# A two-layer gated attention kernel on one core: its loads in the order of use, logarithms beside the first queries, and the ternary layer one unit earlier

## The reference

```python
x = x + tanh(g_xattn[0]) * L0_xattn(layernorm(x), ctx)          # 16 heads of 16, 77 keys
x = x + tanh(g_ffn[0]) * L0_ffn(layernorm(x), w1, w2)           # ternary weights, hidden 1024
x = x + tanh(g_xattn[1]) * L1_xattn(layernorm(x), ctx, distances, ...)
x = x + tanh(g_ffn[1]) * L1_ffn(layernorm(x), ...)              # expert 0, relu, hidden 1024, layer norm
```

## Time and profile before

| | us |
|---|---|
| median of 3 runs | 404.98 (404.76 to 409.9) |
| the profiled execution | 406.22 |
| its span in the trace | 404.5 |
| TensorE busy | 329.9 |
| VectorE busy | 282.7 |
| ScalarE busy | 283.5 |
| GpSimd busy | 230.9 |

### The profile page before, as it was taken

How to read it: one execution, slowest core, us unless ns; L and a number is a source line. 1 busy time by engine, 2 the same in 40 slices (tenths; PEclk the granted TensorE clock), 3 DMA queues, 4 the chain that set the end, 5 groups by cost and what they waited for, 6 DMA issues and landing times.

```text
span 404.5 us, 8923 instructions
## 1 busy us (share of the span) xinstructions
PE 329.9 (82%) x3222; PEld 271.4 (67%) x3222; DVE 282.7 (70%) x676; ACT 283.5 (70%) x516; POOL 230.9 (57%) x413
## 2 busy tenths in 40 slices
PE   2856878878866776878787899899877899999993
PEld 2646767667754453467566688788666799888882
DVE  6895568776777647989955557777856548666665
ACT  4366897799886777989934798866679755555550
POOL 4675644676577222457784755566775167444444
PEclk9996869998998868869999999999999999999998
DMA  8996431011100000320082222211100000000001
GB/s 242 278 179 170 92 86 41 10 39 43 42 6 17 2 0 2 52 25 2 2 257 53 50 53 53 52 35 27 45 2 2 2 0 29 28 28 27 28 28 52
DMA packets 23187, 22.02 MB, mean 54 GB/s; under 512 B 4711, under 2 KB 22504, under 8 KB 23067
## 3 DMA queue, kind: packets, MB, share of 16 engines
q1 hardware_dynamic: 23144, 21.45, 21.5%
HBM read 10.34 MB, written 2.10 MB: 31 GB/s over the span
## 4 chain that ended last, share of the span: by engine, by line
PE 46%; DVE 19%; ACT 17%; issue 10%; POOL 4%; DMA 3%; SPq 1%; ACTq 0%; POOLq 0%; DVEq 0%
PE psA L1723 10%; PE psA L1509 5%; PE psD L1707 5%; PE psBE L1707 4%; PE psD L1418 3%; ACT pp_hi L731 3%; DVE mx L1129 3%; PE psBE L1444 2%; DVE ham L1175 2%; DVE st L885 2%; ACT p L722 2%; PE psA L1493 2%; PE psA L1333 2%; DMA qb<-mT 2%; PE psA L1676 2%
## 5 line engine op out<-in xcount | busy, mean ns | idle before, releaser
L508 POOL TENSOR_TENSOR pp_lo<-p,pp_hi 124x512 f16<-124x512 f32 x80 | 92.7, 1178 | 46.6 <-ACT pp_hi L731 46.6
L404 POOL TENSOR_TENSOR lns<-lns,mhalf 128x2 f32<-128x2 f32 x39 | 31.0, 794 | 86.0 <-DVE lns L890 85.6
L1129 DVE TENSOR_REDUCE mx<-psBE 128x6 f32<-128x462 f32 (+1 forms) x96 | 54.5, 582 | 33.3 <-PE psBE L1444 32.9
L722 ACT ACTIVATE p<-psD 124x512 f32<-124x512 f32 x80 | 47.7, 597 | 27.8 <-PE psD L1418 27.1
L1418 PE MATMUL psD<-qb,ktb 98*124 98x256 f16 (+1 forms) x256 | 49.6, 291 | 12.1 <-DMA qb<-mT 10.3
L731 ACT ACTIVATE pp_hi<-p 124x512 f16<-124x512 f32 x80 | 50.4, 630 | 0.0
L1418 PEld LDWEIGHTS psD<-qb,ktb 98*124 98x124 f16 (+1 forms) x256 | 33.0, 145 | 16.9 <-DMA qb<-mT 13.2
L1444 PE MATMUL psBE<-kt_hi,q_hi 128*128 128x154 f16 (+2 forms) x160 | 34.0, 282 | 5.2 <-ACT mT L713 4.0
L1215 DVE TENSOR_TENSOR pp_lo<-space,pp_hi 128x512 f16<-128x512 f32 x32 | 25.7, 822 | 16.2 <-ACT space L834 15.5
L1723 PE MATMUL psA<-ew_hi,pp_hi 128*128 128x256 f16 x128 | 34.9, 273 | 0.0
L1723 PE MATMUL psA<-ew_hi,pp_lo 128*128 128x256 f16 x128 | 34.9, 273 | 0.0
(11 more groups left out here) (210 smaller groups left out, 1007.3 us busy)
## 6 DMA issues: line engine op xcount, KB each, us to landing
qb<-q_hi SPq DMA_DIRECT2D x32, 128.0 KB
xs<-in_x SPq DMA_DIRECT2D x8, 256.0 KB, 6.0
tw_raw<-in_tw SPq DMA_DIRECT2D x2, 1024.0 KB, 10.2
qb<-q_lo SPq DMA_DIRECT2D x16, 128.0 KB
space<-in_ew SPq DMA_DIRECT2D x2, 1024.0 KB, 6.5
out<-space SPq DMA_DIRECT2D x7, 256.0 KB, 2.1
ktb<-km SPq DMA_DIRECT2D x6, 248.0 KB, 7.9
qb<-bT_lo SPq DMA_DIRECT2D x8, 104.0 KB
```

What stands on the lines that cost most here:

```text
L508: nc.gpsimd.tensor_tensor(pl[:, u % 2, 2 * r:2 * r + 2, :], p32[:, n % 4, :, :], ph[:, u % 2, 2 * r:2 * r + 2, :], ALU.subtract).then_inc( ...
L722: a_(p32[:, n % 4, :, :], psD[n % 2][0:KR, :].rearrange("p (t r) -> p t r", t=2), ACT.Exp, scale=1.0 / SSC).then_inc(a["exp"], 1)
L1129: v.tensor_reduce(pairs[:, MP[k][0]:MP[k][1]:MP[k][2], :], psBE[:, n % 2, 0:hn * KEYS].rearrange("p (q e k) -> p q e k", e=2, k=KEYS), AX. ...
```

## The change

Five things move; no instruction that computes is added or removed (two loads of ACT's function tables are).

- **Loads.** The key weights come before x of unit 0, the query weights before x of unit 1, then distN. distT follows x of unit 2. x of units 5 to 7, the row constants, `wo` and `tw1` go behind the first query blocks, `tw2` behind those of unit 2. The distances have a semaphore each.
- **Logarithms.** `log_distance(0)` stands ahead of the first `queries_hi`, `log_distance(1)` behind `tables_v(0)`.
- **First units.** DVE applies unit 0 before it reads statistics of unit 1, and takes those of unit 2 in slot 0. TensorE's transposes of unit 1 and value table move into slot 0.
- **Ternary layer.** Its unit 0 is taken in halves in slots 8 and 9, unit u in slot 8+u, so that unit 4 falls in slot 12 and the slots of its own begin with 5. ACT's rounding moves from `ternary_second` into the slot (`ternary_rounded`), DVE's `ternary_first` from behind the slot to step 2.
- **Tables of layer 1.** Their steps on DVE and TensorE move back by a slot, two `keys_high` into the first slots of layer 1.

```diff
         def hps(n):
-            return (psD2, psBE)[n % 2][:, :, :].rearrange("p b c -> p (b c)")
+            return (psD2 if n > 0 and n % 2 == 0 else psBE)[:, :, :].rearrange("p b c -> p (b c)")
...
-        d_dist = sem("d_dist")
+        d_dist = [sem(f"d_dist{i}") for i in (0, 1)]
...
+            log_distance(0)
             queries_hi(0, 0)
             ln0_transposed(1)
             tables_v(0)
+            log_distance(1)
             for s in range(NU + 1):
                 attn_slot(0, s)
...
-            for s in range(4):
-                attn_slot(0, NU + 1 + s)
+            for s in range(1, 5):
+                attn_slot(0, NU + s)
                 ternary_second(s)
-            for s in range(4, NU + 1):
+            for s in range(5, NU + 1):
                 ternary_slot(s)
```

ACT, in its slots:

```diff
+                    if l == 0 and (s, r) == (NU + 1, 1):
+                        ternary_hidden(0, (1,))
+                    if l == 0 and (s, r) == (NU + 2, 1):
+                        ternary_transposed(0, (1,))
...
                     if l == 0 and r == 4 and s == NU:
                         tables_v(1)
+                        ternary_hidden(0, (0,))
                     if r == 4 and l == 0 and s > NU:
-                        ternary_hidden(s - NU - 1)
+                        ternary_rounded(s - NU - 1)
+                        ternary_hidden(s - NU)
...
-                if l == 0 and s > NU:
-                    ternary_transposed(s - NU - 2)
+                if l == 0 and s == NU + 1:
+                    ternary_transposed(0, (0,))
+                if l == 0 and s > NU + 1:
+                    ternary_transposed(s - NU - 1)
```

DVE, at the start, in its slots and after them:

```diff
             ln0_stats(0)
-            ln0_stats(1)
             ln0_apply(0, refine(0, SX))
-            ln0_apply(1, refine(1, SX))
             split_keys(0)
             for i in range(2):
                 keys_high(0, i)
+            ln0_stats(1)
             keys_masked(0)
-            ln0_stats(2)
+            ln0_apply(1, refine(1, SX))
...
-                    if r == (1 if s < NU else 0) and 0 <= s - 4 < NU:
+                    if r == (1 if s < NU else 0) and 0 <= s - 4 < (NU - 1, NU)[l]:
                         residual_stats(l, s - 4, ln)
+                    if l == 0 and r == 2 and s > NU:
+                        ternary_first(s - NU - 1)
...
-                if s == 2:
-                    split_keys(1)
+            split_keys(1)
+            tables_v(1, 0)
+            for s in range(5, NU + 1):
+                ternary_slot(s)
+                if s == 5:
                     keys_masked(1)
-                if s == 3:
-                    tables_v(1, 0)
-                    keys_high(1, 0)
-            for s in range(4, NU + 1):
-                ternary_slot(s)
-                if s < 7:
-                    keys_high(1, s - 3)
+                if s in (6, 7):
+                    keys_high(1, s - 6)
             queries_lo(1, 0)
             attn_slot(1, 0, 3 * NU)
             ternary_slot(NU + 1)
+            keys_high(1, 2)
             attn_slot(1, 1, 3 * NU)
             ternary_slot(NU + 2)
+            keys_high(1, 3)
             attn_slot(1, 2, 3 * NU)
```

TensorE, in its slots:

```diff
+                    if l == 0 and s == 0:
+                        if r == 0:
+                            ln0_transposes(1)
+                        if r == 1:
+                            tables_v(0)
...
+                    if l == 0 and (s, r) in ((NU, 3), (NU + 1, 0)):
+                        ternary_hidden(0, (s - NU,))
                     if r == 3 and l == 0 and s > NU:
-                        ternary_hidden(s - NU - 1)
+                        ternary_hidden(s - NU)
```

154 lines of the change are left out of this document (82 added, 72 removed).

## The result

| | before | after |
|---|---|---|
| median, us | 405.88 (20 runs, 401.91 to 409.9) | 408.24 (20 runs, 405.9 to 413.0) |
| ratio | 1 | **1.0075**, 95% interval 1.0055 to 1.0095 |
| profiled execution, its span | 406.22, 404.5 | 410.12, 408.4 |

The change made the kernel 0.75% slower, where 398.2 us were forecast and a range of 392.5 to 403. Nothing was added to explain it: in part 1 of the page TensorE does the same 3222 instructions as in the earlier trace rows, and ScalarE (ACT) two table loads more.

A forecast was written before the change was run, and what follows sets the result against it. The prediction took a chain of waits between engines as the bound. Minus 4.0 (start), minus 3.5 (end of layer) and plus 0.7 (keys) gave minus 6.8: from 404.98 to 398.2 us, own range 395.5 to 401, overall 392.5 to 403.

The forecast's parts named there:

- Start, forecast minus 4.0: Start of layer 0: reordered loads and logarithms bring first scores from 32.48 to 29.0, with a further 0.5 us gained behind.
- a gain of 0.5 for the two together: Behind the first scores: DVE's backlog and a late fourth pp_lo, set against a better clock, net 0.5 us gained.
- the weak bound of the forecast: Smallest gain allowed for the start of layer 0: minus 1.5 us.
- The thin cover of 1 us behind tw1: Unit 1's shift rows queue behind tw1, landing near 40 and needed near 41; the start's bounds hold its loss.
- End of the layer, forecast minus 3.5: End of attention layer 0: ternary work fills ACT's idle time and saves a slot; minus 3.5 us, bounds plus 1 and minus 6.
- slot 12: roundings, then Gelu of unit 4 at 170.5: Step of the walk through ACT: Gelu of unit 4 begins at 170.5, where it began at 173.35 before.
- the walk's minus 4.1: Walk through ACT to slot 12: Gelu of unit 5 at 177.6, where it began at 181.69 before.
- the 1.3 that was forecast: Splitting keys and value tables on DVE a slot later, ahead of the vo matmuls, gives 1.3 us back.
- Keys, forecast plus 0.7, bounds 0 and 1.6: First slots of layer 1: two kt_hi of 0.8 us each move in where DVE sets the pace; plus 0.7 us.
- The slower one: POOL's second power, 5.6 us later, bounds the start and the stall vanishes without gain: 407.8 us; chance 0.05.
- clock rival: Fuller slots remove the idles that lower TensorE's clock; start and end gain 6 us each: 393.7 us; chance 0.20.
- switch rival: A table switch on ACT costs more than its load; two more cost 2.9 us: 401.1 us; chance 0.05.

The follow-up runs named there:

- e15: e7 with TensorE's value tables of slot 0 made three steps later and ACT's copy at the end of slot 0; 0.9947 of the kernel before.
- e18: e7 with 14 transposes of the identity, into a bank nobody reads, ahead of TensorE's first product; 0.986 of the kernel before.
- e7: Changed kernel with tw1 behind unit 1's shift rows, fourth value tables behind unit 7's transposes, high keys in slots 5 to 7, Gelu maxima first; 0.9922 of the kernel before.
- e16: e7 measured again, unchanged, on another chip; 0.9878 of the kernel before.
- e5: Changed kernel with DVE taking the Gelu maxima of units 1 to 3 at the end of their own slot; 1.0007 of the kernel before.
- e1: Changed kernel with the 1 MB load of tw1 behind unit 1's shift rows; 1.0063 of the kernel before.
- e17: e7 without the move of tw1, which goes out ahead of unit 1's shift rows; 0.9847 of the kernel before.
- e2: Kernel before with only the start of the change (loads, logarithms, first units), nothing of the ternary layer; 1.0035 of the kernel before.
- e10: e2 with tw1 behind unit 1's shift rows; 0.9991 of the kernel before.
- e3: Changed kernel with the fourth value tables of layer 1 behind the transposes of unit 7; 1.0048 of the kernel before.
- e12: e7 without the move of the key products, one again ahead of unit 1's maxima in layer 1; 0.9976 of the kernel before.

## Why the prediction was wrong

**Start, forecast minus 4.0.** The step to the first scores held: 29.41, no transfer wait, POOL's second power at 12.95 (forecast 14), first shifts sent at 26.28 where it said 25.4. What failed is the term behind it, "a gain of 0.5 for the two together", which carried the whole gain of the first scores on to the end of the stretch. I took the 8.2 us at a clock of 0.53 for a consequence of the stall, so as something that could only get better. In the 12 traces with the new start whose rows weren't caught (e15 and e18 left out, whose starts differ), stretch a was 112.26 in the mean (108.65 to 114.47), in the three with the old start 113.75: minus 1.5, just the weak bound of the forecast. The low clock that comes at the same time without the stall is the cause that the traces of e7 and e16 point to. The thin cover of 1 us behind tw1, which the prediction named, did give way in the profiled execution and in e5, and costs nothing that e1 and e17 could measure.

**End of the layer, forecast minus 3.5.** The mechanism was right and the walk was on one engine. ACT's events came as written up to slot 11: xTf at 132.19 (forecast 132.1), the end of the second Gelu half at 135.3 (135.0), slot 9 over at 143.64 (143.4), slot 10 at 154.63 (155.5), slot 11 at 166.44 (167.4), with 2.55 us of waits (3). The failed step is the next, "slot 12: roundings, then Gelu of unit 4 at 170.5": it let the roundings follow at once, and they waited 3.07 us for DVE's maximum; that Gelu began at 172.69. The walk didn't follow DVE's queue, in which the residual of unit u-2 now stood ahead of the maximum of unit u.

How much was lost by it is best read from the shifts of unit 7 to the Gelu of unit 5. The old ternary part took 66.33 us there in the mean (the kernel before, e2, e10), the changed one 64.66, the one with the early maxima 61.99. So the walk's minus 4.1 was minus 1.7, and is minus 4.3 once DVE's order is what the walk had assumed (means again; the trace that the walk started from has 67.44). The split of keys and values a slot later cost 1.0 (7.78 us to the next Gelu for 6.74), near the 1.3 that was forecast. In the whole of stretch b the profiled executions say minus 1.6, but the kernel before was itself a high draw: the old part took 81.21, 80.17 (e2) and 78.80 (e10), 80.06 in the mean, against which the changed one gives 0.3 and the one with all moves, which also has the keys in slots 5 to 7, 1.6 (78.47 in the mean of eight).

**What was not in the sum.** The tables of values moved back by a slot. I costed their DVE work (the 1.3 of the split) and not the place of TensorE's fourth step, which ends up in the last slot with nothing behind to hide it: plus 3.04, of which 2.55 go with the step's place (e3). It stood at nothing in the sum without a reason, and is the largest error of the ternary part.

**Keys, forecast plus 0.7, bounds 0 and 1.6.** Measured 2.38 in the changed kernel and three more traces, 0.71 in e5 and e12. The product itself was priced right; what follows it in four of six traces, slower products of TensorE, was outside the bounds.

Together: 0.13 minus 1.63 plus 3.04 plus 2.38 = 3.9 us for a forecast of minus 6.8.

**The rivals.** The slower one named 407.8, close to the result, but by luck. Its sign came: POOL's second power was 4.5 us later (12.95 for 8.42), and the 3.59 us of idle before POOL's first `pp_lo` are gone. Its cost didn't: no idle stretch of TensorE, VectorE or ScalarE between 10 and 74 us ends with POOL, and the losses lie elsewhere. The clock rival's 393.7 has no run that reaches it; e16's profiled execution, with the moves that the rival didn't have, took 397.47. The switch rival is answered: after, xn ends at 128.82, the load takes from 128.84 to 130.12, the exponent starts at 130.13. Of the 1380 ns beside each load in the Trainium skill (ScalarE: Activation LUTs, What ACT_TABLE_LOAD costs) these rows show nothing.

What stays open: whether the move of the keys pays, since time and trace disagree on it, what the two added loads cost by themselves, and what decides the clock.

## What to carry to other kernels

Walk every engine's queue through the moved place, not the one that is to be filled: all three losses of the ternary part were an instruction that stood behind another's wait or work with its own data ready (a maximum behind a residual, transposes behind a table, maxima behind a key product). The same holds for the cure: the key products moved into slots 5 to 7 stand ahead of a maximum there, and that place wasn't walked either. When a pipeline is shifted by one stage, look at the last stage, where what moved has no successor to hide it. And don't book a low clock as the price of the stall ahead of it before a trace without the stall shows it gone.
